# Logits of a unit's first half in one piece, its last transposes behind them, and ScalarE's second pair of exponentials in a row

## The reference

```python
q, k, v = heads(x @ Wq), heads(k_of(x @ Wkv)), heads(v_of(x @ Wkv))   # 16 x 2048 x 64
sim = einsum('bid,bjd->bij', q, k) * scale
G = sigmoid(sim); P = min(reversed_cumsum(G), 63)
sim = sim + (w * E[ceil(P)] + (1 - w) * E[floor(P)])                # E = q @ pos_emb, w = P - floor(P)
attn = softmax(sim); out = attn @ v; out = heads_back(out) @ Wout + b_out
```

## Time and profile before

| | us |
|---|---|
| median of three runs | 2297.18 (2296.54 to 2298.07) |
| the profiled execution, its own time | 2298.53 |
| its span, first to last instruction | 2296.7 |
| TensorE busy | 2230.2 (97%) |
| ScalarE busy | 1762.8 (77%) |
| VectorE busy | 1634.0 (71%) |
| GpSimd busy | 389.3 (17%) |

### The profile page before, as it was taken

How to read it: one execution, slowest core, us unless ns; L and a number is a source line. 1 busy time by engine, 2 the same in 40 slices (tenths; PEclk the granted TensorE clock), 3 DMA queues, 4 the chain that set the end, 5 groups by cost and what they waited for, 6 DMA issues and landing times. The chain is left out here.

```text
span 2296.7 us, 53197 instructions
## 1 busy us (share of the span) xinstructions
PE 2230.2 (97%) x14577; PEld 1449.5 (63%) x14577; DVE 1634.0 (71%) x4269; ACT 1762.8 (77%) x3723; POOL 389.3 (17%) x673
## 2 busy tenths in 40 slices
PE   7999999999999999999999999999999978999997
PEld 5666666666666666666666666666665556777775
DVE  5888888888888888888888888888888801233232
ACT  5888888888888888888888888888888843454453
POOL 1111111111111111111111111111111201121211
PEclk9999999999999999999999999999999989999998
DMA  2010101010101010101010101010102021010100
GB/s 74 24 40 25 39 23 39 23 42 23 40 24 39 23 39 23 39 23 39 23 39 23 39 23 39 23 39 23 34 15 58 12 66 35 28 41 30 39 30 7
DMA packets 109392, 75.44 MB, mean 33 GB/s; under 512 B 28077, under 2 KB 105070, under 8 KB 109294
## 3 DMA queue, kind: packets, MB, share of 16 engines
q1 hardware_dynamic: 109294, 73.95, 11.5%
HBM read 14.33 MB, written 2.10 MB: 7 GB/s over the span
## 5 line engine op out<-in xcount | busy, mean ns | idle before, releaser
L842 DVE TENSOR_REDUCE mx<-Sc 128x1 f32<-128x1024 f32 (+1 forms) x512 | 568.1, 1131 | 246.9 <-PE Sc L632 246.9
L483 ACT ACTIVATE probsT<-rings 128x512 f32<-128x512 f32 x1024 | 554.2, 594 | 196.9 <-PE rings L640 196.5
L640 PEld LDWEIGHTS rings<-ident,probs 128*128 128x128 f32 x4096 | 437.8, 141 | 303.5 <-issue 103.8
L507 ACT ACTIVATE probs<-Sc,nbias 128x1024 f32<-128x1024 f32 x512 | 566.9, 1112 | 29.3 <-DVE nbias L852 29.3
L640 PE MATMUL rings<-ident,probs 128*128 128x128 f32 x4096 | 567.4, 282 | 3.0 <-ACT probs L507 2.5
L632 PE MATMUL Sc<-qk,q_now 64*128 64x512 f32 x2048 | 530.0, 615 | 14.9 <-ACT probs L507 10.5
L654 PE MATMUL out<-probsT,V_now 128*64 128x256 f32 x4096 | 498.3, 386 | 0.0
L805 DVE COPY_PREDICATED z<-mask,z 128x224 f32<-128x224 int16 (+5 forms) x768 | 393.5, 512 | 10.8
L375 POOL TENSOR_TENSOR prod<-cut,z 128x350 f32<-128x350 f32 x128 | 120.7, 943 | 1468.7 <-DVE z L817 1468.7
L654 PEld LDWEIGHTS out<-probsT,V_now 128*64 128x64 f32 x4096 | 271.4, 136 | 153.6 <-issue 42.4
L632 PEld LDWEIGHTS Sc<-qk,q_now 64*128 64x128 f32 x2048 | 177.3, 186 | 120.0 <-issue 104.9
(11 more groups left out here) (128 smaller groups left out, 2261.9 us busy)
## 6 DMA issues: line engine op xcount, KB each, us to landing
q_now<-qk SPq DMA_DIRECT2D x256, 64.0 KB, 2.0
xv<-xT SPq DMA_DIRECT2D x113, 128.0 KB, 2.2
q_far<-qk SPq DMA_DIRECT2D x256, 32.0 KB, 1.8
V_now<-V SPq DMA_DIRECT2D x16, 512.0 KB, 3.0
at<-attn SPq DMA_DIRECT2D x16, 512.0 KB, 3.2
probs<-in_x_dram SPq DMA_DIRECT2D x4, 512.0 KB, 5.5
wqk<-in_L_attn_Wq_dram SPq DMA_DIRECT2D x32, 64.0 KB, 2.0
xin<-in_x_dram SPq DMA_DIRECT2D x16, 128.0 KB, 2.8
```

The source lines that it names most:

```text
L483: nc.scalar.activation(probsT[:, u, 4 * s:4 * s + 4, :], ring[k % 2][:, :].rearrange("p (t q) -> p t q", q=P), ACT.Copy).then_inc(slot_out, 1)
L507: nc.scalar.activation(probs[:, u, cols], Sc[:, cols], ACT.Exp, bias=nbias[:, u:u + 1], accum_out=sums[:, u, half:half + 1]).then_inc(exp_ ...
L640: last = nc.tensor.transpose(ring[k % 2][:, j * P:(j + 1) * P], probs[:, u, (4 * s + j) * P:(4 * s + j + 1) * P], ident[:, :])
L842: nc.vector.tensor_reduce(mx[:, u, half:half + 1], Sc[:, cols], AX.X, ALU.max).then_inc(dve_unit, 1)
```

## The change

On TensorE the second half of tile 0's logits stands straight behind the first, and the two "late" sets of transposes, which stood between them, come behind both. On ScalarE the second exponential of tile 1 stands straight behind the first, ahead of the copies of the halves, of q and k and of V, which it followed before; and the copies of the two "late" sets stand behind `positions` and `distances`, ahead of which they stood. No instruction is added or taken away.

```diff
             def body(g, odd, late=False, ...):                      # ScalarE
                 base = slots_before(g, late)
                 at = Slots()
-                if not first:
-                    transposed(0, base, at.late, (2, 3))
                 if near:
                     positions(g + 1)
                     distances(g + 1)
                 if not first:
+                    transposed(0, base, at.late, (2, 3))
                     transposed(1, base, at.last)
                 exp_half(g, 0, 0)
                 exp_half(g, 0, 1)
...
                 transposed(0, base, at.now, (0, 1))
                 exp_half(g, 1, 0)
+                exp_half(g, 1, 1)
                 if not first:
                     empty_halves(g - 1)
                 if proj:
                     project(g + PAIRS, not odd, base, at.qk, alone=not val)
                 if val:
                     values(g, base, at.values)
-                exp_half(g, 1, 1)
...
                 logits(par, 0, 0)                                   # TensorE
                 if not first:
-                    transposes(0, base, at.late, 2)
-                    transposes(0, base, at.late, 3)
                     wait_apart(pe, exp_done, g * 4, waited)
                 if new_keys:
                     wait_apart(pe, slot_out, base - 1, waited)
                 logits(par, 0, 1)
                 if not first:
+                    transposes(0, base, at.late, 2)
+                    transposes(0, base, at.late, 3)
                     transposes(1, base, at.last, 0)
                     transposes(1, base, at.last, 1)
```

## The result

The changed kernel takes 2330.3 us (median of four runs, 2329.8 to 2331.9) beside 2297.0 for the kernel before (median of four): a ratio of 1.0144, 95% interval 1.0132 to 1.0156. It is slower by 33 us; the forecast was 2326, in 2311 to 2350.

What follows compares the result with a forecast made beforehand. TensorE, busy for 97% of the span, was taken as the bound, held by a two-buffer round trip with ScalarE; 11.8 + 8.8 + 4.9 + 1.7 = 27.2 us on 2298.5 gave 2325.7, rounded 2326, range 2311 to 2350.

Steps and rivals of the forecast that it cites:

- The piece: TensorE: tile 0's logits in one piece of four pairs take 1.92 us, where the two halves took 2.12.
- The round trip: TensorE: first last set waits 1.34 us behind the first late set for its buffer; an ordinary unit is 0.12 longer.
- ScalarE in time: ScalarE: `distances` has ended at 2.54, before the first late copy is wanted at 2.62, so TensorE sets the time.
- the short spacing: ScalarE's small copies: about 0.27 us apart for 256 columns and 0.16 for 128, instead of the present 0.52, 0.44, 0.18.
- Rival C: ScalarE is late because its small copies keep their present spacing: 56 us more, 2355 us; chance 20%.
- First units of a head: Every eighth unit: second half of logits waits for the copy of q and k; first last set at 3.90, costing 0.68.
- The 0.14 for the signal: First units of a head: time from the end of the q and k copy at 1.36 to the logits at 1.50.
- Units 112 to 127: Units with fewer products: second exponential delays logits, first last set at 3.49 against 3.14, costing 0.35 us a unit.
- The sum: All units: 11.8 ordinary, 8.8 first ones, 4.9 last ones, 1.7 for units 112 and 120, together 27.2 us.
- my last paragraph: Signs to look for in the profile after; a granted clock under 1.00 in the units would be an uncounted cost.
- rival A: TensorE: round trip hidden, first last set at 2.85, 0.29 us earlier in an ordinary unit; 2274 us, chance 6%.

Runs made afterwards that it cites:

- q and k first on two buffers: Changed kernel with two buffers, ScalarE copying q and k and V before the halves of the sum: 2324.9 us, ratio 1.0122.
- the turned sums in the gap: Changed kernel with the two matmuls that turn the sum moved between the late and the last sets: 2330.2 us, ratio 1.0138.
- the late copies first: Changed kernel with ScalarE's copies of the late sets put back ahead of `positions` and `distances`: 2422.0 us, ratio 1.054.
- q and k first on three buffers: Changed kernel with a third buffer, ScalarE copying q and k and V before the halves of the sum: 2247.8 us, ratio 0.9790.

## Why the prediction was right

**The piece.** Forecast 1.92, measured 1.94; the second exponential, one behind the other now, was in time for its second half.

**The round trip.** Forecast 1.34 between late and last sets, measured 1.34; first last set at 3.26, measured 3.28; period 14.3, measured 14.31 (641.17 to the next unit at 655.48). The four kernels with two or three buffers and the old or the new order show that this is the cause: the order costs 33 us with two buffers and gives 32 with three.

**ScalarE in time.** I chose the short spacing of the small copies between two ends, and it was 0.27, 0.35 and 0.16. The first late copy starts at 2.63, 0.69 behind its set, where my working had 0.70, and not straight behind `distances`. But it could have started only 0.1 earlier: ScalarE is in time by little. Rival C, with the present spacing, did not come about.

**First units of a head.** Forecast 3.90 for the first last set, measured 3.92. The 0.14 for the signal, for which I had given no row, was 0.14 in unit 40 (the copy of q and k ends at 613.28, the logits start at 613.42). **Units 112 to 127.** Forecast 3.49, measured 3.50.

**The sum.** I compared the distances between the starts of neighbouring units in the two traces, by the median of each kind: 98 x 0.13, 13 x 0.70, 14 x 0.37, and 0.7 and 0.6 for units 112 and 120, together 28 where I had 27. The profiled execution is 32.0 longer. Unit 0 took 1.5 us more than before, by the clock (last section); my last paragraph named a drop of the clock as a cost that I had not counted. Unit 1 took 0.3 more than an ordinary unit, at full clock. The remaining 2 us are waits for DMAs of queries in single units: behind unit 0 TensorE waits 3.8 us for them before and 7.8 after, partly beside other waits. I had counted nothing for any of the three. No step of the sum failed. The forecast loss is 27 us and the measured one 33; what I had left out came to about 4 us in the profiled execution, and that it was so little is luck and not working.

**Where my working was incomplete.** My reading of the earlier trace rows was wrong, though no term of the sum rests on it. I took the 0.8 us of the weight load, 128 times, for a wait for the second buffer, and used it against rival A. With three buffers in the old order the list, in 40 to 1805 us, has the same row:

```profile
PEld rings L649 <- ACT probsT L490: 94.8, 125, 0.8
```

In unit 42 of the kernel before, the copy that this set needs had ended at 630.38, 0.79 before the set starts at 631.17. The weight load has the same 0.8 us before other sets behind logits too, where the list puts it down to the copy of V, to that of q and k, or to nothing ("issue"). What tells of the buffer is TensorE's own wait of 0.25.

That the old order was fully covered at the third and fourth last sets was taken from the sums and is wrong by 0.14 us a unit, as the third buffer in the old order showed. It did not touch the forecast, because both kernels pay it. Rival A's price, 0.29 us an ordinary unit for a hidden round trip, was right: the two orders with three buffers lie 0.30 apart, 32 us in all where A had 24, and the other 15 of the 48 us are the buffer's own.

## What to carry to other kernels

Before two pieces of work are joined to save the gaps between them, ask what the piece that moves away was covering. Here it stood between two users of one buffer, and its 1.06 us, with the 0.9 of the sets, hid a round trip of 1.34 through the other engine; the joined piece saved 0.27 a unit (first last set at 2.87 instead of 3.14 with three buffers) and uncovered 0.41. If a buffer can be found, find it first and join afterwards: the same reordering went from +33 to -32 us.

An engine that is busy for 76% can still have no slack at one place, and two halves of a change may each be slower than the whole: try them together, and read them apart.

## What the runs showed that I had not expected

The first unit of the changed kernel ran at half clock in the profiled execution and at full clock before, with the same instructions and almost the same wait for a DMA in front. The windows of 37.00 to 44.50 us, before and then after (length, busy time of PE, PEld, DVE, ACT, POOL, granted clock, DMA share, GB/s):

```profile
37.00:44.50 7.50, 4.89 (x28) 3.16 (x28) 7.40 (x23) 4.38 (x9) 0.00 (x0) 1.00 0.28 92
```

```profile
37.00:44.50 7.50, 4.82 (x14) 2.17 (x15) 6.58 (x20) 3.41 (x7) 0.00 (x0) 0.59 0.25 92
```

During the wait the granted clock fell to 0.50, the 1.2 GHz level, for 6.8 us, and half as many matmuls fit into the same stretch. TensorE's wait for that DMA was 3.3 us there, and 3.1 in the kernel before, where the clock stayed. Of the other profiled executions, those with TensorE's part alone, with three buffers, with q and k first on two buffers (all three 0.77 in that window) and with the turned sums in the gap (0.64) show it too; those with ScalarE's part alone, with the late copies first, with q and k first on three buffers and with the third buffer in the old order do not (1.00). Two of these four have TensorE's new order, so the order does not bring it by itself. Unit 0 takes 11.74 us in every execution at 1.00 and 13.21 here: it costs about 1.5 us, and which execution has it cannot be told from these runs.

A set that is released at the very moment at which TensorE would start it anyway still costs. In unit 42 of the kernel before, the third and the fourth last set are released by copies that end at 632.46 and 632.94, some 0.05 before they start. The weight load of the third, before and then with three buffers in the old order:

```profile
632.51 0.91 PEld L640 LDWEIGHTS rings<-ident,probs 128*128 128x128 f32 x8
```

```profile
629.34 0.48 PEld L649 LDWEIGHTS ring<-ident,probs 128*128 128x128 f32 x4
```

With the buffer free it starts 0.11 ahead of the set's first transpose (629.45), released just in time it starts with it (632.51). From the third last set to the outputs it is 1.08 in the kernel before and 0.97 with three buffers, from the first to the third 1.34 and 1.32. That is 0.13 of the 0.14 us a unit, 15 us in all, and no list of waits shows it.
